# Fast-weight attention kernel: the state update by 16 products over 128 rows from block-diagonal weighted keys, and solved matrices written with the row index innermost

## The reference, cut to what matters

```python
rk = x.reshape(B, T, H, d);  rk = rk / max(norm(rk), 1e-12)        # keys
wk = rk shifted by one position in time
v = x @ Wv.T;  gate = sigmoid(x @ Wg.T);  beta = sigmoid(x @ Wb.T)
def step(S, inp):                      # S: one 32 x 32 state for each batch and head
    pred = einsum('bhk,bhkd->bhd', wk_t, S)
    err = (v_t - pred) * b_t[..., None]
    S = S + wk_t[..., None] * err[..., None, :]
    o = einsum('bhk,bhkd->bhd', rk_t, S) * g_t[..., None]
out = scan(step) @ Wo.T                # then layer norms, residual, feed-forward
```

## Time and profile before

| | us |
|---|---|
| median of 3 runs (2385.09 to 2395.34) | 2392.36 |
| the profiled execution | 2363.46 |
| its span | 2361.7 |
| PE busy | 2096.4 (89%) |
| DVE busy | 1985.9 (84%) |
| ACT busy | 1726.4 (73%) |
| POOL busy | 1725.6 (73%) |
| q1 (SP's transfers), share of 16 DMA engines | 30.2% |

### The profile page before, as it was taken

One profiled execution on the slowest core, in us unless ns is written; L12 is line 12 of the kernel. 1 busy time (PEld: TensorE's weight loads), 2 busy tenths in 40 slices (PEclk: granted clock), 3 DMA queues, 4 the chain that ended last, 5 costly groups with the idle time before them and its releaser, 6 DMA issues. The chain is left out here.

```text
span 2361.7 us, 145902 instructions
## 1 busy us (share of the span) xinstructions
PE 2096.4 (89%) x61989; PEld 1329.8 (56%) x61989; DVE 1985.9 (84%) x5809; ACT 1726.4 (73%) x3628; POOL 1725.6 (73%) x3096
## 2 busy tenths in 40 slices
PE   1679999999999999999999999999999987399997
PEld 1346666656666666666566666666666655255554
DVE  5388989889888899989888889889888985588886
ACT  2766877778777787787787878778777743477775
POOL 1677888888888888888888888888888853144343
PEclk7789999999999999999999999999999997799999
DMA  2111222222222222222222222222222221478885
GB/s 81 50 49 55 80 74 78 76 76 77 76 76 76 77 76 79 77 77 81 74 78 77 77 73 78 77 75 82 77 76 77 60 60 49 152 198 232 228 230 130
DMA packets 132138, 215.53 MB, mean 91 GB/s; under 512 B 31352, under 2 KB 31360, under 8 KB 131488
## 3 DMA queue, kind: packets, MB, share of 16 engines
q1 hardware_dynamic: 131488, 206.20, 30.2%
HBM read 104.40 MB, written 67.11 MB: 73 GB/s over the span
## 5 line engine op out<-in xcount | busy, mean ns | idle before, releaser
L769 DVE TENSOR_TENSOR ps_elim<-ps_elim,sys 128x30 f32<-128x30 f32 (+14 forms) x1920 | 542.5, 325 | 0.8
L777 DVE TENSOR_TENSOR sys<-sys,ps_elim 128x30 f32<-128x30 f32 (+14 forms) x1920 | 533.9, 315 | 1.0
L894 PE MATMUL ps_v<-wv,xt 128*128 128x512 f16 x1536 | 428.5, 389 | 24.6 <-DMA kbd<-kt 12.6
L894 PE MATMUL ps_y<-wo,ot 128*128 128x512 f16 x1536 | 402.4, 385 | 12.1 <-DVE x L821 9.3
L921 PEld LDWEIGHTS ps_chain<-rhs,t_t 32*32 32x32 f32 x16384 | 263.2, 144 | 127.2 <-issue 125.5
L921 PE MATMUL ps_chain<-rhs,t_t 32*32 32x32 f32 x16384 | 295.0, 218 | 19.9 <-issue 13.9
L678 ACT ACTIVATE state<-ps_s 128x512 f32<-128x512 f32 x128 | 76.4, 597 | 262.2 <-PE ps_s L985 262.1
L915 PEld LDWEIGHTS ps_chain<-state,key_t 32*32 32x32 f32 x16384 | 174.5, 105 | 150.9 <-issue 148.9
L985 PEld LDWEIGHTS ps_s<-err,key_b 32*32 32x32 f32 x16384 | 172.0, 106 | 142.7 <-issue 142.2
L1260 PE MATMUL ps_f<-wq,f_xq 128*128 128x512 f16 x1024 | 242.6, 381 | 6.8 <-DVE f_xq L1232 6.8
L915 PE MATMUL ps_chain<-state,key_t 32*32 32x32 f32 x16384 | 210.8, 195 | 38.2 <-issue 37.7
(11 more groups left out here) (152 smaller groups left out, 5029.1 us busy)
## 6 DMA issues: line engine op xcount, KB each, us to landing
x_in<-in_L_attn_x SPq DMA_DIRECT2D x128, 256.0 KB
kbd<-kt SPq DMA_DIRECT2D x512, 64.0 KB, 2.0
x_res<-in_L_attn_x SPq DMA_DIRECT2D x128, 256.0 KB
x_scratch<-x SPq DMA_DIRECT2D x128, 256.0 KB, 6.4
f_x<-x_scratch SPq DMA_DIRECT2D x32, 1024.0 KB, 7.7
out<-f_res SPq DMA_DIRECT2D x128, 256.0 KB, 3.7
gate<-gates SPq DMA_DIRECT2D x128, 7.9 KB
gate<-gates SPq DMA_DIRECT2D x128, 0.2 KB
```

The lines of the kernel that those rows point to most:

```text
L769: dve.tensor_tensor(tmp, factors(r, c, first, end)[:, c - first:C - 1 - first, c - first:c - first + 1].to_broadcast(shape), sys[:, r, c:c ...
L777: dve.tensor_tensor(dst, dst, tmp, ALU.add).then_inc(elim_done[r], 1)
L894: last = pe.matmul(out, lhs[:, a, kb, :], weights[:, w, kb, :], start=(i == 0), stop=(i == 3 * KB - 1))
```

## The change: what it does

- `update` becomes 16 products, one for each head, over all 128 partitions: weights `kbb` (128 x 128, for each batch b a 32x32 block at rows and columns of b, zero elsewhere), moving operand `err` of that head (128 x 32). They stand in one piece behind 6 output products.
- `kbb` is filled by four DMA transfers a step from `key_b`, one for each batch, of 32 partitions x 16 heads x 32 elements (L449 of the changed kernel), for the tile one step ahead; POOL zeroes it once.
- `key_b` is made at lag 2 in place of 6, and `key_t` at lag 1 in place of 7, at the same places of their engines' steps. `key` now has 8 buffers, `key_t` and `key_b` 2 each.
- `t_t` gets the row index i innermost: DVE writes its blocks with a step of 32 elements, and the weights of a head lie side by side.

```diff
+LAG_KB = 2
+LAG_KT = 1
...
-        key = sb("key", [P, 2, D])
-        key_t = sb("key_t", [P, 8, H, C])
+        key = sb("key", [P, 8, D])
+        key_t = sb("key_t", [P, 2, H, C])
-        key_b = sb("key_b", [P, 8, D])
+        key_b = sb("key_b", [P, 2, D])
+        kbb = sb("kbb", [P, 2, H, B, HD])
-        t_t = sb("t_t", [P, 2, C, 2, H])
+        t_t = sb("t_t", [P, 2, 2, H, C])
...
+                n, l, live = on(base, j, LAG_KT)
+                if live:
+                    if n == 0:
+                        sp.wait_ge(s["kbb_zero"], 1)
+                    wait(sp, s["keyb_done"], n + 1)
+                    wait(sp, s["s_psum"], n - 1)
+                    for b in range(B):
+                        sp.dma_start(kbb[C * b:C * b + C, l % 2, :, b, :],
+                                     heads(key_b[C * b:C * b + C, l % 2, :])).then_inc(kbb_loaded[l % 2], 16)
...
+            pool.memset(kbb[:, :, :, :, :], 0.0).then_inc(s["kbb_zero"], 1)
...
                 n, l, live = on(base, j, LAG_V)
                 if live:
                     wait(pool, s["rn_done"], n + 1)
-                    wait(pool, s["keyt_done"], n - 1)
-                    wait(pool, s["kt_psum"], n - 1)
-                    wait(pool, s["keyb_done"], n - 1)
+                    wait(pool, s["keyt_done"], n - 7)
+                    wait(pool, s["kt_psum"], n - 7)
+                    wait(pool, s["keyb_done"], n - 7)
...
-                    wait(pool, s["s_psum"], n - 7)
...
+                n, l, live = on(base, j, LAG_KB)
+                if live:
+                    wait(pool, kbb_loaded[l % 2], halves(base, j, LAG_KB) * (16 * B))
+                    pool.tensor_tensor(heads(key_b[:, l % 2, :]), heads(key[:, l, :]), spread(gates[:, l, 0:H]),
                                        ALU.mult).then_inc(s["keyb_done"], 1)
...
-                    dve.transpose(t_t[:, r, :, :, :].rearrange("p i a h -> p i (a h)"), sys[:, r, :, :]).then_inc(s["tt_done"], 1)
+                    dve.transpose(t_t[:, r, :, :, :].rearrange("p a h i -> p i (a h)"), sys[:, r, :, :]).then_inc(s["tt_done"], 1)
...
-                n, l, live = on(base, j, LAG_V)
+                n, l, live = on(base, j, LAG_KT)
                 if live:
                     wait(dve, s["key_done"], n + 1)
-                    wait(dve, s["pred_psum"], n - 7)
-                    wait(dve, s["gram_psum"], n - 7)
-                    dve.transpose(key_t[:, l, :, :], heads(key[:, l % 2, :])).then_inc(s["keyt_done"], 1)
+                    wait(dve, s["pred_psum"], n - 1)
+                    dve.transpose(key_t[:, l % 2, :, :], heads(key[:, l, :])).then_inc(s["keyt_done"], 1)
...
-                    wait(pe, s["keyb_done"], n + 1)
+                    wait(pe, kbb_loaded[l % 2], halves(base, j, 0) * (16 * B) + 16 * B)
                     wait(pe, s["err_done"], n + 1)
...
-                output(0, SHARE - 1)
+                output(0, 2 * SHARE - 1)
                 update_ready(base, j)
-                output(SHARE - 1, SHARE)
-                update(0)
-                output(SHARE, 2 * SHARE)
-                last = update(1)
-                if live:
+                output(2 * SHARE - 1, 2 * SHARE)
+                if live:
+                    for h in range(H):
+                        e = slice(HD * h, HD * h + HD)
+                        last = pe.matmul(ps_s[:, e], kbb[:, l % 2, h, :, :].rearrange("p b e -> p (b e)"), err[:, l % 2, e],
+                                         start=(n == 0 and h == 0), stop=True, skip_group_check=True)
                     last.then_inc(s["s_psum"], 1)
```

More of the change, by code:

```diff
@@ L339, in attention @@
         kbd_loaded = [sem(f"kbd_loaded{i}") for i in range(2)]
+        kbb_loaded = [sem(f"kbb_loaded{i}") for i in range(2)]
         gate_done = [sem(f"gate_done{i}") for i in range(8)]
@@ L345, in attention @@
             ss_sum ss_done ln_done rn0_done rn_sq rn_half rn_three rn_done v_psum g_psum v_done gexp_done gden_done gates_done gate_moved
-            key_done keyt_done kt_psum kt_done kbd_zero keyb_done bmask_done gram_psum gram_done mt_done
+            key_done keyt_done kt_psum kt_done kbd_zero kbb_zero keyb_done bmask_done gram_psum gram_done mt_done
             sys_done diag_done tt_done
@@ L485, in step @@
                     wait(pool, s["rn_done"], n + 1)
-                    wait(pool, s["keyt_done"], n - 1)
-                    wait(pool, s["kt_psum"], n - 1)
-                    wait(pool, s["keyb_done"], n - 1)
-                    pool.tensor_tensor(heads(key[:, l % 2, :]), heads(x_hat[:, l % 4, :]), spread(rn[:, l % 2, :]),
+                    wait(pool, s["keyt_done"], n - 7)
+                    wait(pool, s["kt_psum"], n - 7)
+                    wait(pool, s["keyb_done"], n - 7)
+                    pool.tensor_tensor(heads(key[:, l, :]), heads(x_hat[:, l % 4, :]), spread(rn[:, l % 2, :]),
                                        ALU.mult).then_inc(s["key_done"], 1)
@@ L499, in step @@
                                        k["neg_mask"][:, :].unsqueeze(2).to_broadcast([P, C, H]), ALU.mult).then_inc(s["bmask_done"], 1)
-                    pool.tensor_tensor(heads(key_b[:, l, :]), heads(key[:, l % 2, :]), spread(beta),
+                n, l, live = on(base, j, LAG_KB)
+                if live:
+                    wait(pool, kbb_loaded[l % 2], halves(base, j, LAG_KB) * (16 * B))
+                    pool.tensor_tensor(heads(key_b[:, l % 2, :]), heads(key[:, l, :]), spread(gates[:, l, 0:H]),
                                        ALU.mult).then_inc(s["keyb_done"], 1)
@@ L846, in step @@
                     wait(dve, s["keyb_done"], n - 7)
+                    wait(dve, s["bmask_done"], n - 7)
                     wait(dve, s["o_done"], n - 7)
@@ L914, in predict @@
                         for h, q, e in blocks(half):
-                            last = pe.matmul(ps_chain[q, e], key_t[q, l, h, :], state[q, l % 2, e], start=True, stop=True)
+                            last = pe.matmul(ps_chain[q, e], key_t[q, l % 2, h, :], state[q, l % 2, e], start=True, stop=True)
                         return last
@@ L920, in solve_error @@
                         for h, q, e in blocks(half):
-                            last = pe.matmul(ps_chain[q, e], t_t[q, l // 2 % 2, :, l % 2, h], rhs[q, e], start=True, stop=True)
+                            last = pe.matmul(ps_chain[q, e], t_t[q, l // 2 % 2, l % 2, h, :], rhs[q, e], start=True, stop=True)
                         return last
@@ L971, in step @@
                     for kb in range(KB):
-                        last = pe.transpose(ps_v[:, P * kb:P * kb + P], key[:, v_l % 2, P * kb:P * kb + P], k["ident"][:, :])
+                        last = pe.transpose(ps_v[:, P * kb:P * kb + P], key[:, v_l, P * kb:P * kb + P], k["ident"][:, :])
                     last.then_inc(s["kt_psum"], 1)
@@ L980, in output @@
                         return project(ps_y[:, :], ot[:, y_l % 2], k["wo"], range(first, end))
-                def update(half):
-                    if live:
[L984 to L987, removed]
                 if y_live:
```

## The result

The changed kernel took 2613.12 us (median of 4, 2601.41 to 2626.73) against 2392.34 for the kernel before (2385.09 to 2395.34); the ratio is 1.0952, with a 95% interval of 1.0911 to 1.0993. Its profiled execution took 2601.41 us (span 2599.7). Every later comparison stands beside runs of the kernel before on the same chip; their median moved between 2363 and 2395 us, so ratios are used.

What follows compares the result with a forecast made beforehand. SP's queue was taken to bound the changed kernel: 112 steps x 1.72 us = +193, less 7 for the other 16, on 2363.5 gives 2550; with 28.9 to the median, say 2575 us, range 2395 to 2760.

Steps and rivals of the forecast that it cites:

- The sum: Whole kernel: 112 steps x 1.72 us = +193, 16 x -0.4 = -7, on 2363.5 us, plus 28.9 to the median: 2575.
- SP's chain: SP's queue each step: own issues plus gate-transfer wait, 13.25 us, growing by 3.1 for four kbb issues to 16.35.
- the other 16 steps: Steps outside 3 to 114, where x_res, x_in and gates aren't all live: at PE's pace, 16 x -0.4 = -7 us.
- Small packets: kbb's 128 B pieces on the DMA engines: no cost forecast; rival at 83 ns each: 3420 us, chance 0.05.
- The update on PE: PE's 32 update instructions at 60 ns, 1.9 us in place of 1.38: +0.5 us a step (+0.2 to +2.1).
- weight loads decide: Rival on PE: 110 ns an update instruction, SP's issues cheap, PE needs 15.85 us a step: 2550 us, chance 0.10.
- SP's bound: SP's queue sets the step at 16.35 us: 2575 us, own range 2470 to 2780, chance 0.68.
- PE's 0.7 us: PE's solve with t_t's weights side by side: both halves save 0.35 us, -0.7 us; 0 if loads aren't the reason.
- What would show it: Signs: kt waits near none, gate wait near 7 us, step 16.35, update 1.6 to 2.7, solve halves 0.7, PE idle before Gram products.
- The later `key_t` and `key_b`: key_t ready 1.4 us before PE needs it, key_b a step before SP asks: cost 0.
- the second memset: POOL's one-time zeroing, like the first at 3.51 us: 0 to 3.5 us, 0 taken.

Runs made afterwards that it cites:

- in four groups: Changed kernel with kbb transfers issued behind the first gate transfer, its 16 update products split 4 by 4 behind 3, 1, 1 and 1 output products: 1.0206.
- the kernel with the transfers behind the gate: Changed kernel with its four kbb transfers issued between the first gate transfer and the wait for it: 1.0802, 2553 us.

## Why the prediction was right

**The sum.** The step that carried it, SP's chain of 13.25 + 3.1 = 16.35 us, was measured as 16.36. SP's issuing grew by 3.03 us a step where 3.1 was said; the four issues shown took 2.68. The step was 16.67 us, 0.31 above the chain, over 112 steps 35 of the 38 us between 2575 and 2613 us; this is why the kernel was 9.5% slower where 7.6% was said (2575 against 2392). Two smaller errors cancelled: the other 16 steps took some 10 us more and not 7 less, and the median lay 12 us above the profiled execution and not 29. The old update with the transfers kept shows the mechanism by itself.

**Small packets** cost next to nothing, as said: the gate wait behind them rose from 6.96 to 7.04 us.

**The update on PE** was mis-sized: 3.49 us, I took 1.9. I inferred the load from the length of its record (35 ns more for 96 columns) where the spacing of the key transposes, 110 ns, was the measure. SP's longer chain covered the error in the total, by 0.7 us only, which is luck: the sum never asked whether PE would come so near. The rival "weight loads decide" was right in its mechanism and its 110 ns; I had priced it as an alternative to SP's bound, and it stood beside it. PE alone needs 16.0 us, not the 14.2 that I wrote, and 0.8 of that is the lower clock: in four groups at 1.00 it was 15.2.

**The clock** is in no step of mine. It fell in the changed kernel, and cost 5 to 6% in the kernel with the transfers behind the gate, where PE bounds.

**t_t**: PE's 0.7 us came as worked out; that it would show where SP doesn't bound was wrong. Alone, it went for the most part into idle time called "issue", 40 us more in the stretch. The idle time "issue" of 0.8 us a step stood in my first paragraph and I didn't ask what made it.

**What would show it.** SP's slack went and the gate wait stayed at 7 us, and solve took 0.68 us a half; but the 32 update instructions took 3.49 us and not 1.6 to 2.7, and PE's wait came at the output products, behind x_res and DVE's residual, not at the Gram products behind `kbd`. The later `key_t` and `key_b` caused no wait that counts. POOL's first statistics started at 55.65 us, 1.3 later than before (54.34); whether the second memset did that isn't shown, for POOL was idle for 9.56 us between the two.

**Open:** that instruction supply bounds the kernel before is inferred from the burst rate of a stretch alone, measured while the granted clock was 0.50, and from "issue" times that fall with the pairs; it isn't shown by a kernel with fewer pairs and an unburdened SP. With `kbb` issued from another engine's queue it could be, which wasn't tried. Why issues block behind the gate transfer isn't settled, nor how much of the changed kernel's low clock comes from its update and how much from PE's waits.

## What to carry to other kernels

Add up a transfer queue's issues and the waits for its own transfers: that is a chain like an engine's, though it shows in no busy share, and its slack is only what it waits for others. Price a product by the spacing of the nearest rows, not by the length of its record, and don't let one bound hide another: here the transfers (1.0976 with the old update) and the loads of the 16 wide products (1.0206 with the clock kept up) were each enough to make the change a loss. Don't take a wait from the profile at its word when the engine that it names had done its part long before. Ask what PE's "issue" time is before counting on a shorter product.

## What the runs showed of the hardware that I had not expected

- f32 products with 128 weights take 109 ns an instruction at 32 columns and 112 at 128; 32x32 ones 10.6 (64 of a solve in 0.68 us).
- The granted clock fell to 0.50 under f32 products with 128 weights and 48 columns, with PE busy all the time, and held at 1.00 with 160 columns; one dense f16 product between groups of 8 of the update's instructions kept it at 1.00 here.
- PE's instructions came in packets of 128 pairs, one in 3.7 us on average in a stretch of small products alone, at a granted clock of 0.50.
- The first `kbb` issue on SP's queue right behind a gate transfer of 127 rows took up to 6.7 us, against a median of 0.63.
- DVE's transpose of 1024 columns took 1926 ns when it wrote with a step of 32 elements, 1188 when it wrote contiguously.
